# A recurrent layer on eight cores: layer-norm statistics in a pass of their own, eight PSUM banks for the projections, and half of the final stores from SP

## Chip, cores and metric

The kernel runs on all 8 cores of one Trainium2 chip. There are 2 sequences of 4096 tokens with 2048 channels; each core computes 1024 tokens of one sequence and reads 128 tokens (and one more) ahead of them, so that no core needs another's result. The metric is the device time in microseconds of the slowest core.

## What is computed

All weight matrices are 2048 x 2048. After a layer norm of x, the layer mixes each token with the one before it, makes four projections, runs a decaying scan over time, multiplies the result with two sigmoids, projects it again, normalises once more, and multiplies with a feed-forward branch whose weights are rounded to -1, 0 or 1.

```python
xn = _layernorm(x)
prev = jnp.concatenate([xn[:, 1:2, :], xn[:, :-1, :]], axis=1)
xx = prev - xn
r = (xn + xx * tm_r) @ Wr.T
k = (xn + xx * tm_k) @ Wk.T
v = (xn + xx * tm_v) @ Wv.T
g = sigmoid((xn + xx * tm_g) @ Wg.T)
w = exp(-exp(time_decay))
# scan over t:  ek = exp(k_t); out = (a + e^u*ek*v_t) / (b + e^u*ek)
#               a = w*a + ek*v_t;  b = w*b + ek
attn = sigmoid(r) * wkv
o = attn * g @ Wo.T
mu = o.mean(-1); var = ((o - mu) ** 2).mean(-1)
s = (o - mu) * rsqrt(var + 1e-5) * ln_g + ln_b
out = x + s * silu(xn @ ternary(W_ffn) + bias)
```

## The kernel before

Channels lie on the partitions (16 tiles of 128 channels, `CH` = 16) and the core's 1024 tokens (`T_OWN`) in the free dimension, as two chunks of 512 (`TC_OWN`). The program is a row of blocks. In a block each engine has its own hand-written list of instructions, and counting semaphores order them; a new block starts when all engines are through with the one before. All weights come from HBM in f32 and are cast to bf16 by ACT or VectorE (DVE) on the way into `wbf`.

The blocks are these. (1) Statistics of x: ACT makes an f16 copy and an f16 square of each tile, PE sums both over the partitions by matmuls with a column of ones. (2) Normalisation and mixing, the inputs of the projections written to HBM. (3) The projections k and v and the feed-forward branch, in `mm_group`. (4) The block that the change is mainly about (from line 732 on), called the rgo block here. (5) The final block (from line 1048 on).

The rgo block does three projections of 32 output groups each: p = 0 the receptance r (weights `wr`), p = 1 the gate g (`wg`), p = 2 the output o (`wo`). A group is 128 output channels by 512 tokens: 16 matmuls, one for each input tile, into one PSUM bank `ps[g % NBK]`, with NBK = 6 banks. Weights come in slabs of 512 output channels, four slabs to a projection and eight groups to a slab. Two slabs fit in `wbf`. SP loads a slab's 16 pieces of 128 x 512 f32 into two staging buffers `rgo_mw` (line 848), and ACT casts each (line 832, `emit_cast`). The cast of slab s+2 may start when PE is done with slab s, and it stands in ACT's list ahead of the first eviction of slab s+1. So ACT's order in a slab is: 16 casts, then eight evictions (lines 968, 975 and 978), each waiting for its group. PE waits before a group until ACT has evicted the group six before it.

During r, DVE also runs the scans, and ACT the Ln and Exp that make a reciprocal (lines 959, 961), two evictions apart. In the gate projection DVE multiplies each evicted chunk into `wkv_sb` (line 917), and PE starts the output projection only when all of that is done.

In the output projection ACT copies each group into `sr_sb` (line 978). After the second chunk of a channel tile it also makes that tile's f16 copy `oh16` (line 984) and f16 square `oq16` (line 986), two buffers of each. PE sums them over the partitions with four matmuls of a column of ones (`stats_mm`, lines 998 and 1001) into two more PSUM banks, `qsa` and `qsb`, one row per chunk. `stats_mm` of a tile stands in PE's list two tiles (four groups) later. At the end of the block DVE reads the sums and makes mean and variance, and ACT the reciprocal square root with Ln and Exp (lines 923 to 936 and 991 to 993).

```python
if (p == 2 and tj == ntc - 1
        and 0 <= sl * OSL + oc - 2):
    stats_mm(e, sl * OSL + oc - 2)
```

The final block broadcasts the two rows of statistics over the partitions (lines 1069 to 1091). Then for each of 16 channel tiles DVE scales and shifts o (lines 1123, 1126), ACT applies ln_g and ln_b (line 1097), and DVE multiplies with the feed-forward branch and adds x (lines 1110, 1113) into one of two buffers `outst`. SP loads x and the branch for tile ci (`xst`, line 1079; `g2ld`, line 1083) when tile ci-2 is done. POOL stores every tile to y (line 1136), and DVE waits before line 1110 for the store of the tile two before.

Of the kernel before, what the change touches and what calls it, by code (L numbers as in the profile page):

```python
# [8 lines left out]
F32 = mybir.dt.float32  # L9
# [6 lines left out]
LN_EPS = 1e-5  # L16
# [7 lines left out]
def build_nc(C, T_OWN, LANE):  # L24
# [15 lines left out]
           for k in ("wk", "wv", "wr", "wg", "wo", "wf")}  # L40
# [18 lines left out]
           ("sl", "sw0", "sw1", "scv", "scs", "smm", "sm2", "sev", "st0",  # L59
            "st1", "sv", "ss", "sden", "srd", "sg0", "sg1")}  # L60
# [633 lines left out]
    with contextlib.ExitStack() as es:  # L694
# [14 lines left out]
                     for i in range(8)]}  # L709
# [12 lines left out]
    oh16 = [es_o.enter_context(nc.sbuf_tensor("oh16_%d" % i, [128, T_OWN],  # L722
                                              F16)) for i in range(2)]
    oq16 = [es_o.enter_context(nc.sbuf_tensor("oq16_%d" % i, [128, T_OWN],
                                              F16)) for i in range(2)]
    stv = es_o.enter_context(nc.sbuf_tensor("stv", [1, T_OWN], F32))
    stm = es_o.enter_context(nc.sbuf_tensor("stm", [1, T_OWN], F32))
    stq = es_o.enter_context(nc.sbuf_tensor("stq", [1, T_OWN], F32))
# [3 lines left out]
    with contextlib.ExitStack() as es:  # L732
# [21 lines left out]
              for i in range(6)]  # L754
        qsa = ec(nc.psum_tensor("qsa", [128, 512], F32))
        qsb = ec(nc.psum_tensor("qsb", [128, 512], F32))
        qs1 = [qsa[32 * j:32 * j + 1, :] for j in range(len(TC_OWN))]
        qs2 = [qsb[32 * j:32 * j + 1, :] for j in range(len(TC_OWN))]
# [108 lines left out]
        def _(e):  # L867
# [53 lines left out]
            e.wait_ge(sem["sm2"], b["sm2"] + CH)  # L921
            for j, (t0, t1) in enumerate(TC_OWN):
                e.tensor_scalar(stm[:, t0:t1], qs1[j][:, :t1 - t0],  # L923
                                1.0 / C, None, OP.mult)
                e.tensor_scalar(stv[:, t0:t1], qs2[j][:, :t1 - t0],
                                1.0 / C, None, OP.mult)
            e.drain()
            e.tensor_tensor(stq[:, :], stm[:, :], stm[:, :], OP.mult)
            e.drain()
            e.tensor_tensor(stv[:, :], stv[:, :], stq[:, :], OP.subtract)  # L930
            e.drain()
            inc(e.tensor_scalar(stv[:, :], stv[:, :], LN_EPS, None,
                                OP.add), "sv")
            e.wait_ge(sem["ss"], b["ss"] + CH + 1)
            e.drain()
            inc(e.tensor_tensor(stm[:, :], stm[:, :], stv[:, :], OP.mult),
                "sv")
# [266 lines left out]
```

## Time and profile before

| | us |
|---|---|
| timed runs: lowest, median, highest of 2 | 1530.3, 1541.25, 1552.21 |
| the profiled execution, its own time | 1497.94 |
| its span, first to last instruction of the slowest core (core 4) | 1496.4 |
| spans of the eight cores | 1465.2 to 1496.4 |
| busy in that span: PE / DVE / ACT / POOL | 823.4 / 524.8 / 496.7 / 105.1 |

All times in the text are microseconds from the start of core 4's span, unless another core is named. By them the rgo block goes from 768 to 1394 (r to 1028, gate to 1210, output to 1380, then the end of the statistics) and the final block from there to the end. In the rows, PE is TensorE's matmuls, PEld its weight loads, DVE VectorE, ACT ScalarE, POOL GpSimd and SPq the DMA issues of SyncE. L1025 is line 1025 of the kernel. A row of a timeline is one instruction, or a run of equal ones (x96) with the time from the first to the end of the last; in brackets stands the engine's idle time ahead of it and what ended that.

### The profile page before, as it was taken

What the parts mean: (1) busy time and instruction counts of PE and PEld (TensorE: products, weight loads), DVE (VectorE), ACT (ScalarE), POOL (GpSimd) and SP (SyncE); (2) the same over time, 40 slices, a digit from 0 to 9 for tenths busy, and PEclk for the clock granted to TensorE, in tenths of its full rate; (3) what the DMA queues carried; (4) which work ended last, traced back from release to release, by engine and by line L of the source; (5) the groups of instructions that cost most, each with busy time, mean ns of one, the idle gap of its engine ahead of it and who ended that gap; (6) DMA issues with size and microseconds to landing.
All of it is one profiled execution on the core that took longest, in us unless ns stands there. A gap on an engine that the chain in (4) does not pass through costs nothing. (4 is left out here: it accounts for less than half of the span.)

```text
span 1496.4 us, 11814 instructions; the slowest of 8 cores (1465.2 to 1496.4 us)
## 1 busy us (share of the span) xinstructions
PE 823.4 (55%) x3834; PEld 359.4 (24%) x3834; DVE 524.8 (35%) x499; ACT 496.7 (33%) x660; POOL 105.1 (7%) x196
## 2 busy tenths in 40 slices
PE   3542210057938479999921758433766777569200
PEld 0110000023514145544410323111323332223000
DVE  0159998100000002765015149667100000000597
ACT  4532222112121121121212446745533235444221
POOL 0002222000000000011110001000000000000000
PEclk8555555578969689999975888676889998779555
DMA  4448879773361842654145443345333332320287
GB/s 128 126 149 261 264 244 261 164 228 113 109 164 53 249 123 90 182 165 140 39 148 175 120 128 111 98 145 172 85 113 110 94 100 76 85 85 1 83 253 226
DMA packets 79070, 211.65 MB, mean 141 GB/s; under 512 B 11424, under 2 KB 11424, under 8 KB 79008
## 3 DMA queue, kind: packets, MB, share of 16 engines
q1 hardware_dynamic: 54432, 139.57, 33.8%
q0 software_dynamic: 15360, 53.49, 9.9%
q10 hardware_dynamic: 9216, 17.83, 3.9%
q8 instruction: 31, 0.51, 0.1%
q14 instruction: 31, 0.25, 0.1%
HBM read 166.81 MB, written 39.85 MB: 138 GB/s over the span
## 5 line engine op out<-in xcount | busy, mean ns | idle before, releaser
L1025 PE MATMUL rgo_ps<-mov_rg,rgo_wbf 128*128 128x512 bf16 x1024 | 245.1, 405 | 204.5 <-ACT sr_sb L968 79.0
L405 PE MATMUL g1ps<-mov_kv,g1wbf 128*128 128x512 bf16 (+1 forms) x1536 | 259.5, 334 | 116.5 <-DMA mov_kv<-sxk 46.8
L832 ACT ACTIVATE rgo_wbf<-rgo_mw 128x512 bf16<-128x512 f32 x192 | 119.5, 629 | 273.8 <-DMA rgo_mw<-wr 89.7
L405 PEld LDWEIGHTS g1ps<-mov_kv,g1wbf 128*128 128x128 bf16 x1536 | 132.6, 100 | 243.3 <-issue 126.9
L1025 PEld LDWEIGHTS rgo_ps<-mov_rg,rgo_wbf 128*128 128x128 bf16 x1024 | 105.0, 103 | 344.6 <-issue 239.0
L1025 PE MATMUL rgo_ps<-wkv_sb,rgo_wbf 128*128 128x512 bf16 x512 | 116.9, 388 | 1.7 <-DVE wkv_sb L917 1.7
L405 PE MATMUL g1ps<-xn_sb,g1wbf 128*128 128x512 bf16 x512 | 110.8, 379 | 3.7 <-DVE g1wbf L266 3.7
L269 DVE CAST g1wbf<-g1mwstg 128x1024 bf16<-128x1024 f32 x24 | 16.7, 694 | 251.2 <-PE g1ps L405 94.7
L333 ACT ACTIVATE g1row<-g1ps 128x512 f16<-128x512 f32 (+1 forms) x96 | 44.5, 492 | 147.1 <-PE g1ps L405 135.4
L573 PE MATMUL ps_sc<-fs_a,ones 128*1 128x512 f16 x64 | 32.3, 609 | 86.9 <-ACT fs_a L618 86.9
L271 ACT ACTIVATE g1wbf<-g1mwstg 128x1024 bf16<-128x1024 f32 x24 | 25.4, 1056 | 127.6 <-DMA g1mwstg<-wv 76.3
L1025 PEld LDWEIGHTS rgo_ps<-wkv_sb,rgo_wbf 128*128 128x128 bf16 x512 | 49.9, 100 | 69.2 <-issue 14.5
L405 PEld LDWEIGHTS g1ps<-xn_sb,g1wbf 128*128 128x128 bf16 x512 | 50.0, 98 | 64.1 <-issue 4.1
L923 DVE TENSOR_SCALAR stm<-qsa 1x512 f32<-1x512 f32 x2 | 1.4, 680 | 172.8 <-PE qsb L1001 172.8
L618 ACT ACTIVATE fs_a<-g1mwstg 128x1024 f16<-128x1024 f32 x32 | 33.7, 1057 | 83.9 <-DMA g1mwstg<-wf 83.9
L901 DVE TENSOR_TENSOR wkv_sb<-r_vvr,r_ekr 128x1024 bf16<-128x1024 f16 x16 | 11.1, 692 | 136.6 <-ACT r_ekr L961 135.7
L917 DVE TENSOR_TENSOR wkv_sb<-wkv_sb,rgo_sg 128x512 bf16<-128x512 bf16 x32 | 13.6, 425 | 115.9 <-ACT rgo_sg L975 113.8
L340 ACT ACTIVATE g1g2s<-g1ps,v_bfv,scale_sb 128x512 bf16<-128x512 f32 x32 | 24.9, 777 | 85.5 <-PE g1ps L405 82.8
L261 DVE TENSOR_SCALAR g1mwm<-g1mwstg,thr_sb 128x1024 f32<-128x1024 f32 x32 | 24.1, 755 | 81.2 <-PE g1ps L405 52.0
L515 PE MATMUL ps<-xh,ones 128*1 128x512 f16 (+1 forms) x48 | 24.0, 499 | 34.7 <-ACT xq L502 34.7
L883 DVE TENSOR_TENSOR_SCAN zar<-w_sb,r_vvr 128x1152 f32<-128x1152 f32 x16 | 41.0, 2560 | 1.5 <-issue 0.4
L1136 POOL DMA_DIRECT2D y<-outst x16 | 8.5, 533 | 462.1 <-DVE outst L1113 462.1
(112 smaller groups left out, 861.4 us busy)
## 6 DMA issues: line engine op xcount, KB each, us to landing
g1mwstg<-wf SPq DMA_DIRECT2D x64, 512.0 KB, 5.0
g1mwstg<-wk SPq DMA_DIRECT2D x32, 512.0 KB, 7.2
g1mwstg<-wv SPq DMA_DIRECT2D x32, 512.0 KB, 5.0
rgo_mw<-wr SPq DMA_DIRECT2D x64, 256.0 KB, 3.3
rgo_mw<-wg SPq DMA_DIRECT2D x64, 256.0 KB, 3.3
rgo_mw<-wo SPq DMA_DIRECT2D x64, 256.0 KB, 3.4
xstg<-x SPq DMA_DIRECT2D x16, 576.5 KB, 3.8
xst<-x SPq DMA_DIRECT2D x16, 512.0 KB, 4.8
```

The lines of the kernel that those rows point to most:

```text
L261: e.tensor_single_scalar(mwm2[jj % 2][:, :], mwstg[jj % 2][:, :], thr_sb[:, :], OP.is_gt)
L269: e.tensor_copy(dstsl, mwstg[jj % 2][:, :]).then_inc(sem["scv"], 1)
L271: e.activation(dstsl, mwstg[jj % 2][:, :], AF.Copy).then_inc(sem["scs"], 1)
L333: inc(e.activation(rowst[ro % 2][:, t0:t1], bank[:, :t1 - t0], fn), "sev")
L340: inc(e.activation(g2st[gk % 2][:, :t1 - t0], bank[:, :t1 - t0], AF.Silu, bias=s["bias_vec"][:, ocg:ocg + 1], scale=scale_sb[:, 0:1]), "sev")
L405: mm = e.matmul(bank[:, :t1 - t0], wbf[hh % 2][:, ic, oc * 128:(oc + 1) * 128], s["mov"][:, ic, t0:t1], start=(ic == 0), stop=(ic == CH - 1))
L515: e.matmul(ps1[j][:, :t1 - t0], ones16[:, :], xh16[:, ci, t0:t1], start=(ci == 0), stop=(ci == CH - 1))
L573: mm = e.matmul(ps_sc[:, :q1 - q0], ones16[:, :], habs[sl_ % 2][:, q0:q1], start=(sl_ == 0 and j == 0), stop=(sl_ == NSL - 1 and j == len( ...
L618: inc(e.activation(habs[sl_ % 2][:, :], g1mwstg[sl_ % 2][:, :], AF.Abs), "scv")
L832: e.activation(wbf[ss % 2][:, ic, :], mwstg[jj % 2][:, :], AF.Copy).then_inc(sem["scs"], 1)
L883: e.tensor_tensor_scan(zar[:, 1:], wbc, vvr[m][:, :], 0.0, OP.mult, OP.add)
L1025: mm = e.matmul(bank[:, :t1 - t0], wbf[ss % 2][:, ic, oc * 128:(oc + 1) * 128], phs[p]["mov"][:, ic, t0:t1], start=(ic == 0), stop=(ic == ...
```

## The change

Four things change. The statistics leave the rgo block and get a block of their own behind it; the work in it is the same, tile by tile, with the same two buffers. The two PSUM banks that this frees go to the projections: NBK is 8. The semaphore `sm2` is gone and `smm` takes its part. In the final block the odd tiles are stored by SP (semaphore `sg0`), the even ones by POOL as before. The buffers of the statistics are allocated in the last part of the kernel.

```diff
         ps = [ec(nc.psum_tensor("rgo_ps%d" % i, [128, 512], F32))
-              for i in range(6)]
-        qsa = ec(nc.psum_tensor("qsa", [128, 512], F32))
-        qsb = ec(nc.psum_tensor("qsb", [128, 512], F32))
...
+              for i in range(8)]
...
                     inc(e.activation(sr_sb[:, ocg, t0:t1], bank[:, :t1 - t0],
                                      AF.Copy), "sev")
-                    if tj == ntc - 1:
-                        if ocg >= 2:
-                            e.wait_ge(sem["sm2"], b["sm2"] + ocg - 1)
-                        e.drain()
-                        e.activation(oh16[ocg % 2][:, :], sr_sb[:, ocg, :],
-                                     AF.Copy)
-                        inc(e.activation(oq16[ocg % 2][:, :],
-                                         sr_sb[:, ocg, :], AF.Square), "ss")
...
-                            if (p == 2 and tj == ntc - 1
-                                    and 0 <= sl * OSL + oc - 2):
-                                stats_mm(e, sl * OSL + oc - 2)
-            stats_mm(e, OSL * NSLAB - 2)
-            stats_mm(e, OSL * NSLAB - 1)
...
+            blk = esA.enter_context(nc.Block())
+            b = snap()
+
+            @blk.scalar
+            def _(e):
+                for ci in range(CH):
+                    if ci >= 2:
+                        e.wait_ge(sem["smm"], b["smm"] + ci - 1)
+                    e.activation(oh16[ci % 2][:, :], o_sb[:, ci, :], AF.Copy)
+                    inc(e.activation(oq16[ci % 2][:, :], o_sb[:, ci, :],
+                                     AF.Square), "ss")
...
+            @blk.tensor
+            def _(e):
+                for ci in range(CH):
+                    e.wait_ge(sem["ss"], b["ss"] + ci + 1)
+                    for j, (t0, t1) in enumerate(TC_OWN):
+                        e.matmul(ps1[j][:, :t1 - t0], ones16[:, :],
+                                 oh16[ci % 2][:, t0:t1],
+                                 start=(ci == 0), stop=(ci == CH - 1))
+                        mm = e.matmul(ps2[j][:, :t1 - t0], ones16[:, :],
+                                      oq16[ci % 2][:, t0:t1],
+                                      start=(ci == 0), stop=(ci == CH - 1))
+                    inc(mm, "smm")
...
                     inc(e.dma_start(g2ld[ci % 2][:, :], sg2[ci, :, :]),
                         "sw%d" % (ci % 2), 16)
+                    k = ci - 2
+                    if k >= 1 and k % 2 == 1:
+                        e.wait_ge(sem["sden"], b["sden"] + k + 1)
+                        inc(e.dma_start(y_d[k, :, :], outst[k % 2][:, :]),
+                            "sg0", 16)
...
-                    stp = "st%d" % (ci % 2)
+                    stp = "st0" if ci % 2 == 0 else "sg0"
...
-                for ci in range(CH):
+                for ci in range(0, CH, 2):
                     e.wait_ge(sem["sden"], b["sden"] + ci + 1)
                     inc(e.dma_start(y_d[ci, :, :], outst[ci % 2][:, :]),
-                        "st%d" % (ci % 2), 16)
+                        "st0", 16)
```

On ACT, in the output projection before, the second set of casts, the evictions behind it (`sr_sb<-rgo_ps`) and the f16 copies and squares (`oh`, `oq`) stand like this:

```order
L832 ACTIVATE rgo_wbf<-rgo_mw 128x512 x16
L978 ACTIVATE sr_sb<-rgo_ps 128x512 x2
L984 ACTIVATE oh_0<-sr_sb 128x1024
L986 ACTIVATE oq_0<-sr_sb 128x1024
L978 ACTIVATE sr_sb<-rgo_ps 128x512 x2
L984 ACTIVATE oh_1<-sr_sb 128x1024
L986 ACTIVATE oq_1<-sr_sb 128x1024
```

And in the changed kernel, from the last set of casts over the block boundary into the statistics:

```order
L821 ACTIVATE rgo_wbf<-rgo_mw 128x512 x16
L950 ACTIVATE sr_sb<-rgo_ps 128x512 x16
L725 UNCONDITIONAL_BRANCH
L1008 UNCONDITIONAL_BRANCH
L1013 ACTIVATE oh_0<-sr_sb 128x1024
L1014 ACTIVATE oq_0<-sr_sb 128x1024
L1013 ACTIVATE oh_1<-sr_sb 128x1024
L1014 ACTIVATE oq_1<-sr_sb 128x1024
```

The copies and squares have moved from between the evictions to behind all of them.

On PE, the output projection (`rgo_ps<-wkv_sb`) before, with the sums of the first two tiles among its groups:

```order
L1025 MATMUL rgo_ps<-wkv_sb,rgo_wbf 128x512 x96
L998 MATMUL qsa<-oh_0,ones 1x512
L1001 MATMUL qsb<-oq_0,ones 1x512
L998 MATMUL qsa<-oh_0,ones 1x512
L1001 MATMUL qsb<-oq_0,ones 1x512
L1025 MATMUL rgo_ps<-wkv_sb,rgo_wbf 128x512 x32
L998 MATMUL qsa<-oh_1,ones 1x512
```

And now, the whole of the gate and r projections in the first row and the whole output projection in the second:

```order
L974 MATMUL rgo_ps<-mov_rg,rgo_wbf 128x512 x1024
L974 MATMUL rgo_ps<-wkv_sb,rgo_wbf 128x512 x512
L725 UNCONDITIONAL_BRANCH
L1022 UNCONDITIONAL_BRANCH
L1027 MATMUL qs_0<-oh_0,ones 1x512
L1030 MATMUL qs_0<-oq_0,ones 1x512
L1027 MATMUL qs_1<-oh_0,ones 1x512
L1030 MATMUL qs_1<-oq_0,ones 1x512
```

Nothing stands between the output groups any more, and the sums follow behind a block boundary.

On SP, the end of the final block before (the loads of the last two tiles):

```order
L1079 DMA xst<-x 128x1024
L1083 DMA g2ld<-sg 128x1024
L1079 DMA xst<-x 128x1024
L1083 DMA g2ld<-sg 128x1024
L1048 UNCONDITIONAL_BRANCH
```

And now, with the stores of tiles 13 and 15:

```order
L1086 DMA xst<-x 128x1024
L1090 DMA g2ld<-sg 128x1024
L1086 DMA xst<-x 128x1024
L1090 DMA g2ld<-sg 128x1024
L1095 DMA y<-outst 128x1024
L1100 DMA y<-outst 128x1024
L1055 UNCONDITIONAL_BRANCH
```

A store of an odd tile has come in behind the two loads of the tile after next, and the last one closes SP's list.

## Rows read from the trace of the kernel before

**Rows 1.** Cores: span and mean granted TensorE clock of core 4.

```profile
core 4: 1496.4 us, clock 0.754
```

**Rows 2.** Windows of core 4: busy by engine (instructions), granted clock, DMA share, GB/s.

```profile
145.00:330.00 185.00, 32.96 (x110) 9.93 (x111) 112.49 (x98) 40.23 (x42) 31.39 (x59) 0.53 0.82 235
...
1085.00:1210.00 125.00, 89.60 (x384) 38.71 (x382) 10.60 (x25) 43.02 (x75) 0.00 (x0) 0.86 0.35 101
1210.00:1380.00 170.00, 125.19 (x572) 51.50 (x572) 0.04 (x1) 76.09 (x110) 0.00 (x0) 0.86 0.26 72
```

**Rows 3.** Timeline of ACT in the gate projection: evictions, then the next casts.

```profile
1157.64 3.02 ACT L975 ACTIVATE rgo_sg<-rgo_ps 128x512 bf16<-128x512 f32 x6
1164.22 0.60 ACT L975 ACTIVATE rgo_sg<-rgo_ps 128x512 bf16<-128x512 f32 x1 [3.57 <-PE rgo_ps L1025]
1167.68 0.60 ACT L975 ACTIVATE rgo_sg<-rgo_ps 128x512 bf16<-128x512 f32 x1 [2.86 <-PE rgo_ps L1025]
1168.17 1.14 ACT L832 ACTIVATE rgo_wbf<-rgo_mw 128x512 bf16<-128x512 f32 x2
```

**Rows 4.** Lines, 1085 to 1210: busy, mean ns, idle before and its releaser.

```profile
L975 ACT ACTIVATE rgo_sg<-rgo_ps 128x512 bf16<-128x512 f32 x25 | 13.2, 602 | 21.5 <-PE rgo_ps L1025 21.5
```

**Rows 5.** Timeline of PE at the start of the output projection.

```profile
1210.40 20.88 PE L1025 MATMUL rgo_ps<-wkv_sb,rgo_wbf 128*128 128x512 bf16 x96 [1.68 <-DVE wkv_sb L917]
1244.14 0.59 PE L998 MATMUL qsa<-oh,ones 128*1 128x512 f16 x2 [12.86 <-ACT oq L986]
...
1245.09 8.48 PE L1025 MATMUL rgo_ps<-wkv_sb,rgo_wbf 128*128 128x512 bf16 x32
```

**Rows 6.** Timeline of ACT in the receptance projection: first casts after the evictions.

```profile
918.72 1.15 ACT L832 ACTIVATE rgo_wbf<-rgo_mw 128x512 bf16<-128x512 f32 x2
```

**Rows 7.** Timeline of ACT, output projection: first cast and first eviction of each slab.

```profile
1209.36 1.14 ACT L832 ACTIVATE rgo_wbf<-rgo_mw 128x512 bf16<-128x512 f32 x2
...
1240.85 1.07 ACT L978 ACTIVATE sr_sb<-rgo_ps 128x512 bf16<-128x512 f32 x2
...
1256.27 1.13 ACT L832 ACTIVATE rgo_wbf<-rgo_mw 128x512 bf16<-128x512 f32 x2
...
1289.49 1.07 ACT L978 ACTIVATE sr_sb<-rgo_ps 128x512 bf16<-128x512 f32 x2
...
1304.48 1.13 ACT L832 ACTIVATE rgo_wbf<-rgo_mw 128x512 bf16<-128x512 f32 x2
...
1336.10 1.07 ACT L978 ACTIVATE sr_sb<-rgo_ps 128x512 bf16<-128x512 f32 x2
```

**Rows 8.** Timeline from the last statistics pair to the final block.

```profile
1379.93 1.06 ACT L984 ACTIVATE oh<-sr_sb 128x1024 f16<-128x1024 bf16 x1
1380.89 1.04 ACT L986 ACTIVATE oq<-sr_sb 128x1024 f16<-128x1024 bf16 x1
...
1382.80 0.68 DVE L923 TENSOR_SCALAR stm<-qsa 1x512 f32<-1x512 f32 x1 [172.76 <-PE qsb L1001]
...
1392.40 1.21 DVE L936 TENSOR_TENSOR stm<-stm,stv 1x1024 f32<-1x1024 f32 x1 [3.70 <-ACT stv L993]
1393.89 0.33 SPq L1079 DMA_DIRECT2D xst<-x  x1
```

**Rows 9.** Timeline of PE, 80 to 100: four matmuls with the ones column.

```profile
92.34 1.96 PE L573 MATMUL ps_sc<-fs_a,ones 128*1 128x512 f16 x4 [1.63 <-ACT fs_a L618]
```

**Rows 10.** Final block: instructions and waits of `outst`; one load's and one store's issue.

```profile
L1110 DVE TENSOR_TENSOR outst<-sstg,g2ld x16: 1224/1225/1226, 1410.6 to 1488.4; 128x1024 f32<-128x1024 f32 x16
...
  DMA y<-outst: 2.3, 4
...
DMA to landing us min/median/max: 3.0/6.5/7.5
...
1418.80 0.57 SPq L1083 DMA_DIRECT2D g2ld<-sg  x1
1418.95 0.54 POOL L1136 DMA_DIRECT2D y<-outst  x1 [4.66 <-DVE outst L1113]
```

More of the change, by code:

```diff
@@ L721, in build_nc @@
     es_o = contextlib.ExitStack()
[L722 to L728, printed above, removed]
     sr_sb = es_o.enter_context(
@@ L920, in _ @@
                                         OP.mult), "sv")
[L921 to L926, printed above, removed]
-            e.drain()
[L928 to L937, printed above, removed]
         @blk.scalar
@@ L1042, in build_nc @@
         ec = es.enter_context
+        oh16 = [ec(nc.sbuf_tensor("oh16_%d" % i, [128, T_OWN], F16))
+                for i in range(2)]
+        oq16 = [ec(nc.sbuf_tensor("oq16_%d" % i, [128, T_OWN], F16))
+                for i in range(2)]
+        stv = ec(nc.sbuf_tensor("stv", [1, T_OWN], F32))
+        stm = ec(nc.sbuf_tensor("stm", [1, T_OWN], F32))
+        stq = ec(nc.sbuf_tensor("stq", [1, T_OWN], F32))
         rb2 = ec(nc.sbuf_tensor("rb2", [128, T_OWN], F32))
@@ L1046, in build_nc, with _ @@
                for i in range(2)]
+        with contextlib.ExitStack() as esA:
+            ecA = esA.enter_context
+            ps1 = [ecA(nc.psum_tensor("qs1_%d" % j, [1, 512], F32))
+                   for j in range(len(TC_OWN))]
+            ps2 = [ecA(nc.psum_tensor("qs2_%d" % j, [1, 512], F32))
+                   for j in range(len(TC_OWN))]
+            blk = esA.enter_context(nc.Block())
[8 more added lines that the diff above has]
+                                     AF.Square), "ss")
+                e.wait_ge(sem["sv"], b["sv"] + 1)
+                e.activation(stv[:, :], stv[:, :], AF.Ln)
+                e.drain()
+                inc(e.activation(stv[:, :], stv[:, :], AF.Exp, scale=-0.5),
+                    "ss")
+            @blk.tensor
[10 more added lines that the diff above has]
+                    inc(mm, "smm")
+            @blk.vector
+            def _(e):
+                e.wait_ge(sem["smm"], b["smm"] + CH)
+                for j, (t0, t1) in enumerate(TC_OWN):
+                    e.tensor_scalar(stm[:, t0:t1], ps1[j][:, :t1 - t0],
+                                    1.0 / C, None, OP.mult)
+                    e.tensor_scalar(stv[:, t0:t1], ps2[j][:, :t1 - t0],
+                                    1.0 / C, None, OP.mult)
+                e.drain()
+                e.tensor_tensor(stq[:, :], stm[:, :], stm[:, :], OP.mult)
+                e.drain()
+                e.tensor_tensor(stv[:, :], stv[:, :], stq[:, :], OP.subtract)
+                e.drain()
+                inc(e.tensor_scalar(stv[:, :], stv[:, :], LN_EPS, None,
+                                    OP.add), "sv")
+                e.wait_ge(sem["ss"], b["ss"] + CH + 1)
+                e.drain()
+                inc(e.tensor_tensor(stm[:, :], stm[:, :], stv[:, :], OP.mult),
+                    "sv")
@@ L1084, in _ @@
                         "sw%d" % (ci % 2), 16)
+                    k = ci - 2
[3 more added lines that the diff above has]
+                            "sg0", 16)
+                for k in range(max(1, CH - 2), CH):
+                    if k % 2 == 1:
+                        e.wait_ge(sem["sden"], b["sden"] + k + 1)
+                        inc(e.dma_start(y_d[k, :, :], outst[k % 2][:, :]),
+                            "sg0", 16)
+                e.wait_ge(sem["sg0"], cnt["sg0"])
             @blk.scalar
```

22 lines of the change are left out of this document (2 added, 20 removed).

## Prediction, made before the changed kernel was run

> **What bounds the kernel now.** I read the cores first: the spans are close together (core 4 is the longest of 1465.2 to 1496.4 us) and TensorE was granted three quarters of its clock on average [rows 1]. No core is special. Then the busy times by stage: in the gate stage (1085 to 1210 us) and the output stage (1210 to 1380) PE is busy for 90 of 125 and 125 of 170 us, ACT for 43 and 76, DMA at 35% and 26% [rows 2]. Nothing is full there; two waits alternate. The ACT timeline shows how [rows 3]: after 16 casts of a weight slab come six evictions in 3.02 us, then 3.57 and 2.86 us of waiting for PE with one eviction behind each, then at once the next casts, at 1168.17. PE had stopped, because ACT evicts nothing while it casts and PE owns six banks: six groups, 20.88 us [rows 5], and it is out. Groups seven and eight start only after the casts, and the next casts only after them.
>
> **Part 1: eight banks in the gate stage.** With eight banks PE does a slab's eight groups under the casts. Six groups take 20.88 us, 3.48 each; two after a stall take 8.48 instead of 6.96 [rows 5]; so eight take 27.8 + 1.5 = 29.4 us. They start about 0.5 us after the casts of the slab before, when the first bank is free, and ACT asks for the results 4.0 us (eight evictions at 0.5) plus a set of casts later (from 1168.17 to 1209.36 a slab takes 41.2 us; less 6.4 of waiting and 4 of evictions that is 31): PE has 4 to 5 us to spare. What goes is ACT's wait for PE, 21.5 us over the stage in one row [rows 4], of which 3.57 + 2.86 = 6.4 lie in the slab shown. What is late next is the casts' own loads, which the change doesn't touch: a slab then costs 31 + 4 = 35 us. In the receptance stage before (818 to 1028 us) I cost the banks at nothing: ACT runs casts, Ln/Exp pairs with their table loads and sigmoids there without a gap, and the next casts start with no idle time ahead of them [rows 6], so PE is not waited for. **Term: -21.5 us** (ends 0 and -21.5: the wait cannot shrink below nothing).
>
> **Part 2: the output stage without the statistics.** Before, it runs from the first cast at 1209.36 to the end of the last eviction at 1379.9: 170.6 us [rows 7, 8]. In it are three sets of casts, from the rows 31.5, 33.2 and 31.6 us, 96.3 together [rows 7]. Between two sets lie eight evictions, four pairs of ACTIVATE for the statistics and PE's groups seven and eight, which PE starts only after the statistics matmuls that stand ahead of them: it waits 12.86 us for `oq` [rows 5]. After the change: 96.3 for the casts, two sets of eight evictions at 4.0, then the last slab: 0.5 until its first bank is free, 29.4 for its groups, 0.7 for the last eviction. 96.3 + 8.0 + 0.5 + 29.4 + 0.7 = 134.9 us. **Term: 134.9 - 170.6 = -35.7 us.** The pairs' removal is in this term.
>
> **Part 3: the statistics by themselves.** Before, 2.9 us lie between the start of the last pair and DVE's first read of the sums (1379.93 to 1382.80) [rows 8]. After, a block boundary comes first. Its price I take from the one that follows: DVE's last multiply ends at 1392.40 + 1.21, SP's first load starts at 1393.89, 0.3 us. Then 16 pairs on ACT alone. A pair's halves last 1.06 and 1.04 us and start 0.96 us apart, so a pair takes 1.91; 15 pairs 28.7 us, and the last one with its matmuls 2.9 as now. 0.3 + 28.7 = +29.0 us more than before. That holds with matmuls at the higher clock level. At the lower one (1.2 GHz) four matmuls of this shape last 1.96 us [rows 9], and with two `oh`/`oq` buffers the loop from a copy to the copy two tiles on is 0.96 + 1.04 + 1.96 + 0.2 of signalling = 4.16 us instead of 3.82: 16 x 0.17 = 2.7 us, and 1 us at the end. Ends +29.0 and +32.7. I take **+29.7 us**, near the warm end, since the pass starts warm from the last slab.
>
> The Trainium skill speaks to both parts on one page ("Perfetto Trace Analysis", Optimization Strategy). It advises interleaving regimes whose most-contended engine differs; the change undoes just that, and by this rule alone it would lose the pass, some 30 us. The same section says that the same gap coming back on an engine can mean too little PSUM for the next tile, and the ACT and PE rows are such a gap [rows 3, 5]. By the rows the second outweighs the first here.
>
> **Part 4: the odd stores.** In the last stage DVE is the limit: its first operation on a tile comes every 5.19 us (1410.6 to 1488.4, 15 steps), each of its four takes 1.23, and it waits only 2.3 us in all for a store [rows 10]. The eight odd tiles' stores move from POOL to SP, behind both loads of tile k+2, on the ring that carries those loads. POOL issued at 1418.95; SP is free of its second load at 1419.37, so the store goes 0.4 us later. Nobody is held up behind it: SP's next loads wait for DVE's next tile. DVE needs the buffer two tiles less two operations after the add, 10.4 - 2.5 = 7.9 us, 7.4 after POOL's issue; stores land 3.0 to 7.5 us after it, median 6.5 [rows 10]. So this is near an edge. Ends: -2.8 us (every wait for a store gone, and half a microsecond at the last store, which is odd and leaves SP at once) and +14 (the ring serves the store after the loads: 0.9 of issue, 6 for the loads, 3.0 for the store, 9.9 us against 7.9 allowed, 2 us for each of seven). **Term: -0.5 us**, the last store alone, because the bytes stay the same and DVE keeps its 5.2 us a tile.
>
> The skill's "DMA: Bandwidth & Descriptors" (Issuing engines are not separate DMA queues) says that transfers of all issuing engines run on the same 16 engines and a second issuer saves issue time only. By it the bandwidth gain of part 4 is zero; no row here shows a store from SP.
>
> **Sum.** -21.5 - 35.7 + 29.7 - 0.5 = -28.0 us. The profiled execution took 1497.9 us, so it would take 1469.9. The two timed runs took 1530.3 and 1552.2, 32 to 54 more, for a reason that the trace does not hold. The terms are sums of fixed counts of instructions, so I take the same 28.0 from the median 1541.25: 1513.2 us, 1.8% less. Faster or slower by 2%, 30.8 us, is about what a measurement of this kernel can tell from no change.
>
> **Rivals.** *A, the small terms fall well*: the statistics matmuls stay warm (+29.0), the store waits go (-2.8). -21.5 - 35.7 + 29.0 - 2.8 = -31.0, 1510.2 us, just past 2%. For it: each term is inside its bounds. Against: it needs both.
> *B, the stores on SP's ring hold up DVE*: +14 instead of -0.5, so -13.5 us, 1527.7. For it: the slowest store already lands when it is needed. Against: on one ring a store no longer shares its turn with the loads that follow it.
> *C, the loads set the slab's length; this one ends slower.* A slab is 16 loads of 256 KB, 4.19 MB: 102 GB/s in the 41.2 us of now, 120 in 35. If eight cores cannot load faster than they do now, the casts stretch until a slab takes as long as before. Then the gate term is gone and, of the output term, its first two slabs: from cast to cast 46.9 and 48.2 us against 35.5 and 37.2 after the change, 22.4 us. The last slab's 13.3 stays: -13.3 + 29.7 - 0.5 = +15.9, 1557.2 us. It decides from 28 / 7 = 4 us of stretch in each of the seven sets of casts. Against it: the core moved 101 GB/s in the gate stage, and 235 at 145 to 330 us, where the other cores loaded too [rows 2]. To reach 2% slower it must also meet B.
> *D, PE is too slow for the banks to help*: at the lower level a group of 16 matmuls would take about twice 3.48 us and eight 56, longer than the casts. Against: the pair after a stall loses 1.5 us in all [rows 5], so it is back at the higher level within a group. Its price would be above that of C.
>
> **Chances.** My forecast 0.50, A 0.25, B 0.12, C and D 0.08, others 0.05. Faster by over 2% is A and a quarter of the forecast, which lies 2.8 us from the line: 0.38. Slower by over 2% takes the worst of C and D: 0.05. The rest, 0.57, is within 2%. The executions seen differ by 54 us among themselves; so the range goes from the midpoint of the profiled and the lowest timed run less the gain, 1514 - 28 = 1486, to B with 12 us of the same spread, 1540.
>
> **What would show it.** Right: in the gate stage 16 casts, eight evictions in 4.0 us, casts again, no wait for PE, slabs 35 us apart; an output stage of about 135 us; a statistics stretch of about 31 us with ACT back to back; DVE's tile still 5.2 us in the last stage. Wrong: sets of casts of 35 us or more (C); waits of DVE for `y` above 1 us on odd tiles (B); ACT waiting for PE in the statistics stretch (the cold end of part 3); groups of 7 us (D).

## The result, and the profile after

| | before | after |
|---|---|---|
| timed, median (runs) | 1495.61 (10) | 1462.36 (11) |
| lowest to highest | 1489.41 to 1552.21 | 1447.38 to 1503.14 |
| profiled execution, its own time | 1497.94 | 1465.46 |
| its span, slowest core | 1496.4 | 1463.9 |
| its span, median of the eight cores | 1476.4 | 1445.1 |

The changed kernel takes 0.9731 of the time before, interval 0.9690 to 0.9773: 2.7% faster, some 40 us. The forecast was 1513.2 with a range from 1486 to 1540; the measured 1462.4 lies outside it. The gain was forecast as 28 us. The base it was taken from, 1541.25, was the median of two runs (1530.3 and 1552.2) that turned out to be the two highest of ten. In some executions two to four cores of one die run 20 to 80 us longer than the others, at granted clocks down to 0.69 (six of 57 later executions of the kernel before took 1529 to 1554 us in this way), and the ratios leave such disturbed executions out, four of the changed kernel's eleven here, which is why the ratio says 40 us where the medians of all runs differ by 33.

The gate stage on ACT in the changed kernel, from the timeline of core 4 (start, duration, engine, line and operation); the rows with single casts between are left out. It answers to [rows 3]:

```profile
1118.89 4.00 ACT L947 ACTIVATE rgo_sg<-rgo_ps 128x512 bf16<-128x512 f32 x8
1122.70 1.21 ACT L821 ACTIVATE rgo_wbf<-rgo_mw 128x512 bf16<-128x512 f32 x2
...
1153.24 4.00 ACT L947 ACTIVATE rgo_sg<-rgo_ps 128x512 bf16<-128x512 f32 x8
1157.05 1.21 ACT L821 ACTIVATE rgo_wbf<-rgo_mw 128x512 bf16<-128x512 f32 x2
...
1187.43 4.00 ACT L947 ACTIVATE rgo_sg<-rgo_ps 128x512 bf16<-128x512 f32 x8
```

Eight evictions stand in one row of 4.00 us, with no bracket ahead of them: ACT found its groups done each time. Before there were six and then two waits. From one first eviction to the next it is 34.4 and 34.2 us; the prediction said 35.

The output projection on PE, and its end on ACT, same core. It answers to [rows 5, 7]:

```profile
1192.57 29.64 PE L974 MATMUL rgo_ps<-wkv_sb,rgo_wbf 128*128 128x512 bf16 x128 [8.44 <-ACT rgo_wbf L821]
1222.45 27.79 PE L974 MATMUL rgo_ps<-wkv_sb,rgo_wbf 128*128 128x512 bf16 x128 [0.23 <-ACT sr_sb L950]
1256.87 29.92 PE L974 MATMUL rgo_ps<-wkv_sb,rgo_wbf 128*128 128x512 bf16 x128 [6.63 <-ACT sr_sb L950]
1290.65 29.47 PE L974 MATMUL rgo_ps<-wkv_sb,rgo_wbf 128*128 128x512 bf16 x128 [3.87 <-ACT sr_sb L950]
```

PE now does a whole slab, 128 matmuls, in one stretch of 27.8 to 29.9 us (29.4 was forecast), where it broke off after 96. It waits for ACT only between slabs. The windows of core 4 for the gate stage, the output stage, the statistics and the final block (busy time and count by engine, granted clock, DMA share, GB/s), beside [rows 2]:

```profile
1088.00:1191.00 103.00, 82.44 (x358) 35.78 (x356) 11.18 (x27) 41.73 (x74) 0.00 (x0) 0.91 0.40 123
1191.00:1321.00 130.00, 116.82 (x512) 51.11 (x512) 1.02 (x3) 46.43 (x81) 0.00 (x0) 0.94 0.33 93
1321.00:1355.00 34.00, 18.45 (x64) 4.71 (x64) 0.64 (x2) 31.77 (x33) 0.00 (x0) 0.90 0.00 0
1376.00:1464.00 88.00, 0.00 (x0) 0.00 (x0) 77.98 (x64) 19.84 (x16) 4.27 (x8) 0.50 0.72 221
```

The output stage takes 130 us for the matmuls that took 170; its rate of loading rises from 72 to 93 GB/s because the same bytes move in less time. The third row is the new pass: ACT busy for 31.8 of 34 us, and the DMA engines idle. How it begins and ends, with the rows that answer to [rows 8]:

```profile
1320.22 0.60 ACT L950 ACTIVATE sr_sb<-rgo_ps 128x512 bf16<-128x512 f32 x1 [2.86 <-PE rgo_ps L974]
...
1321.08 1.28 ACT L1013 ACT_TABLE_LOAD   x1 [0.26 <-PEq L725]
1322.38 1.06 ACT L1013 ACTIVATE oh<-sr_sb 128x1024 f16<-128x1024 bf16 x1
...
1326.49 1.06 ACT L1013 ACTIVATE oh<-sr_sb 128x1024 f16<-128x1024 bf16 x1 [0.22 <-PE qs L1030]
...
1354.36 0.68 DVE L1039 TENSOR_SCALAR stm<-qs 1x512 f32<-1x512 f32 x1 [162.16 <-PE qs L1030]
...
1360.26 1.06 ACT L1017 ACTIVATE stv<-stv 1x1024 f32<-1x1024 f32 x1 [7.17 <-DVE stv L1048]
...
1362.59 1.21 DVE L1052 TENSOR_TENSOR stm<-stm,stv 1x1024 f32<-1x1024 f32 x1 [2.42 <-ACT stv L1019]
...
1364.07 0.33 SPq L1086 DMA_DIRECT2D xst<-x  x1
```

Between the last eviction and DVE's first read lie 33.5 us. ACT waits for PE once, for 0.22 us. A table load (ACT loading its function tables) that the prediction had not counted stands ahead of the first copy; in exchange the one ahead of the logarithm (line 991 before) is gone, and the row work up to the last multiply is 1.4 us shorter.

Each stage's length, as the median of the eight cores, in us. "r" is the time up to the end of the receptance evictions; "statistics" runs from the last eviction to DVE's first read of the sums; "rows" is the mean and variance work; "tail" is from DVE's last add to the end of the span. The medians need not add up.

| | r | gate | output | statistics | rows | broadcast, final | tail |
|---|---|---|---|---|---|---|---|
| before | 1011.2 | 180.1 | 167.2 | 2.9 | 10.8 | 98.0 | 5.3 |
| after | 1013.1 | 158.2 | 129.6 | 33.6 | 9.4 | 98.6 | 3.0 |
| difference | +1.9 | -21.9 | -37.6 | +30.7 | -1.4 | +0.6 | -2.3 |
| forecast | 0 | -21.5 | -35.7 | +29.7 | 0 | 0 | -0.5 |

### The profile page after: what moved, and what is told of

It is laid out like the page before. It is cut to its first block and busy times, and to the rows that moved or that the text cites. A ratio compares the mean times of both kernels' runs of the same rounds, so it can differ in the third digit from the quotient of the medians.

```text
span 1463.9 us, 11807 instructions; the slowest of 8 cores (1437.9 to 1463.9 us)
## 1 busy us (share of the span) xinstructions
PE 827.9 (57%) x3834; PEld 362.3 (25%) x3834; DVE 524.4 (36%) x499; ACT 494.0 (34%) x660; POOL 101.8 (7%) x188
## 5 line engine op out<-in xcount | busy, mean ns | idle before, releaser
L974 PE MATMUL rgo_ps<-mov_rg,rgo_wbf 128*128 128x512 bf16 x1024 | 235.8, 395 | 189.7 <-ACT rgo_wbf L821 121.5
L269 DVE CAST g1wbf<-g1mwstg 128x1024 bf16<-128x1024 f32 x24 | 16.7, 694 | 246.6 <-PE g1ps L405 94.4
L515 PE MATMUL ps<-xh,ones 128*1 128x512 f16 (+1 forms) x48 | 24.0, 499 | 34.2 <-ACT xq L502 34.2
L874 DVE TENSOR_TENSOR_SCAN zbr<-w_sb,r_ekr 128x1152 f32<-128x1152 f32 x16 | 40.5, 2533 | 0.0
```

The source lines that it names most:

```text
L515: e.matmul(ps1[j][:, :t1 - t0], ones16[:, :], xh16[:, ci, t0:t1], start=(ci == 0), stop=(ci == CH - 1))
L874: e.tensor_tensor_scan(zbr[:, 1:], wbc, ekr[m][:, :], 0.0, OP.mult, OP.add)
L974: mm = e.matmul(bank[:, :t1 - t0], wbf[ss % 2][:, ic, oc * 128:(oc + 1) * 128], phs[p]["mov"][:, ic, t0:t1], start=(ic == 0), stop=(ic == ...
```

## The experiments

Unless it says otherwise an edit is made to the changed kernel. "Median core" is the median of the eight cores' spans, averaged over the executions that the ratio keeps; where profiles are named, it is that of the one profiled execution. Why it is used follows from the next three runs. A stage's length is always its median over the cores in the profile.

### The same programs again: three runs on the base

No edit, twice the changed kernel and once the kernel before.

> The changed kernel once more, beside the kernel before on one chip, to size the effect by cores and not by the slowest one alone. Theory F (the step times of the profiles are the whole effect): the median over the eight cores falls by what the two profiled executions differ, 1476.4 - 1445.1 = 31 us, and the time of the slowest core by 31 to 33. Rival N (the slowest core is picked by chance among eight, and the before-kernel's slowest core stands out more): the median core falls by 31, the slowest by about 40, as in the timed runs so far (1495 to 1455).

Measured: 1459.65 against 1490.16, ratio 0.9816 [0.9754, 0.9879]: 1.8% faster, not 2.7% as in the first comparison. The median core went from 1472.5 to 1440.3, 32.2 less. The stages repeat the first profile's within some 3 us (output 132.8, gate 159.6, statistics 33.5).

> The kernel before, unchanged, against itself, to see what this measurement calls a difference, and to have its eight cores' spans in timed runs. If the timed effect of the change (27 us on one chip, 40 on another) is larger or smaller than the 31 us of the median core only by chance of the slowest core, the ratio is 1 within 0.8%, the median core lies at 1473 to 1478 us in each fast run and the slowest core 10 to 25 us above it. Rival: the timed runs' median core stands apart from the profiled one's, by more than 5 us; then the profile understates the effect.

Measured: 1493.34 against 1493.04, ratio 0.9992 [0.9949, 1.0036]. A program against itself comes out within half a per cent, so neither 0.9731 nor 0.9816 comes from the way of comparing.

> The changed kernel a third time, beside the run of the kernel before against itself. Step times of the profiles: median core 31 us under that of before, fast runs' ratio 0.979 +- 0.006. Rival (an effect of 40 us as in the first comparison): 0.973 or less.

Measured: 1460.19 against 1493.04, ratio 0.9801 [0.9761, 0.9841]; median core 1444.6 against 1475.4, 30.8 less. The three comparisons give gains of 40, 27 and 30 us by the slowest core, and 31 to 32 by the median core (profiles and the last two). The slowest core lies 3 to 25 us above the median one, and it is another core from run to run: at the median 10 us in 39 executions of the kernel before, and 15 in 19 of the changed one. So the kernel's own gain is 31 us; what the timed metric adds or takes is that scatter. Whether the gain passes 2% stays open: of the three intervals only the first lies wholly beyond it. The median of the kernel before is 1487 to 1496 in all four comparisons (the fourth stands beside the later experiments); only single executions reach 1541.

### Six and seven banks

```diff
-              for i in range(8)]
+              for i in range(6)]
```

and `range(7)` in the second.

> The changed kernel with six banks for the projections instead of eight; everything else as changed. Theory F (the banks carry the gain, the split costs): ACT waits for PE again in each slab, 6.4 us. Against the changed kernel +2.2 + 3 x 6.4 in the gate stage = +21, and in the output stage two slabs at +6.4 and the last with groups seven and eight of the slab before still to do, +7: +20. So about 41 us slower than the changed kernel, and 2 to 9 us slower than the kernel before. Rival S (taking the statistics out from between the output groups is what pays, because ACT and PE no longer wait for each other there): the output stage stays within 10 us of the changed kernel's 130 us and the kernel is at least 20 us faster than before.

> The changed kernel with seven banks. Theory F: one group, 3.5 us, is left outside the casts in each slab, but ACT's first seven evictions (3.5 us) overlap the start of it; per slab 16 casts, seven evictions, a wait of 2.9 to 4 us for the eighth group, one eviction: +3.5 us a slab against eight banks. Six slabs with a next set of casts, 3.5 each, and 3.5 in the last: +21 to +25 us against the changed kernel. Rival E (seven are enough, since the wait ends when ACT starts evicting and PE has 4 to 5 us to spare): within 5 us of the changed kernel.

Six banks: 1502.64, ratio 1.0123 [1.0063, 1.0183]: slower than the kernel before. Against the changed kernel the median core is 39.4 longer in the profiles, of which 20.4 in the gate stage and 20.9 in the output stage. The waits are back in ACT's timeline (core 1):

```profile
1151.93 3.02 ACT L947 ACTIVATE rgo_sg<-rgo_ps 128x512 bf16<-128x512 f32 x6
1158.83 0.60 ACT L947 ACTIVATE rgo_sg<-rgo_ps 128x512 bf16<-128x512 f32 x1 [3.89 <-PE rgo_ps L974]
1162.29 0.60 ACT L947 ACTIVATE rgo_sg<-rgo_ps 128x512 bf16<-128x512 f32 x1 [2.86 <-PE rgo_ps L974]
1162.78 1.14 ACT L821 ACTIVATE rgo_wbf<-rgo_mw 128x512 bf16<-128x512 f32 x2
```

Seven banks: 1483.47, ratio 0.9926 [0.9873, 0.9979], the gate stage 10.4 and the output stage 10.6 longer than with eight. Each bank is worth 10 us in each stage, and rivals S and E fall. This splits the change: the banks give -41, and moving the statistics out (with the odd stores from SP), with no bank gained for it, would by itself have cost about 10 us (+30.8 for the pass, -1.4 in the rows, -2.3 in the tail, and 167.2 to 150.5 = -16.7 in the output stage; the span medians say +8). The timed runs put both higher: their median core is 1489.3 with six banks, in three executions, which makes -49 for the banks and +17 for the rest. The split is known to some 10 us, the sum of 31 better.

### The kernel before with a seventh bank

The four rows of sums go into one bank, and the freed one to the projections.

```diff
-              for i in range(6)]
+              for i in range(7)]
...
-        qsb = ec(nc.psum_tensor("qsb", [128, 512], F32))
...
-        qs2 = [qsb[32 * j:32 * j + 1, :] for j in range(len(TC_OWN))]
+        qs2 = [qsa[64 + 32 * j:65 + 32 * j, :] for j in range(len(TC_OWN))]
```

> The kernel BEFORE with one edit: the four rows of statistics share one PSUM bank (rows 0, 32, 64, 96), and the projections have seven banks. The statistics stay between the output groups. Theory O (order): the gate stage falls by 10 us, as from six to seven banks in the changed kernel, but the output stage does not move, because in PE's list the sums of a tile whose copy ACT makes only after the casts stand ahead of the seventh group: PE stops after six groups whatever the banks. So 10 us less than before. Rival P (banks alone): the output stage falls by 10 us too, 20 us less than before.

Measured: 1473.91, ratio 0.9893 [0.9848, 0.9937], median core 1462.4 against 1475.2. So this small edit alone gives some 13 us. The gate stage is 13.4 shorter, the output stage only 2.5: rival P falls. The same bank is worth 10.3 in the output stage once the statistics are out (140.2 against 150.5). PE's timeline of core 4 shows why:

```profile
1184.49 20.88 PE L1024 MATMUL rgo_ps<-wkv_sb,rgo_wbf 128*128 128x512 bf16 x96 [1.69 <-DVE wkv_sb L916]
1217.48 0.58 PE L997 MATMUL qsa<-oh,ones 128*1 128x512 f16 x1 [12.11 <-ACT oq L985]
1217.48 0.59 PE L1000 MATMUL qsa<-oq,ones 128*1 128x512 f16 x1
1217.48 0.58 PE L997 MATMUL qsa<-oh,ones 128*1 128x512 f16 x1
1217.49 0.59 PE L1000 MATMUL qsa<-oq,ones 128*1 128x512 f16 x1
1218.01 9.31 PE L1024 MATMUL rgo_ps<-wkv_sb,rgo_wbf 128*128 128x512 bf16 x32
```

PE has a free bank after 96 matmuls and still stops for 12 us: next in its list stand the statistics of a tile whose square ACT makes only after its casts. The list's order stops it, and no bank helps there. So a bank and the removal of the statistics are worth more together than apart; that is shown for the seventh bank, not for the eighth, for which the interleaved form has no room.

### All stores from POOL again

```diff
-                    k = ci - 2
-                    if k >= 1 and k % 2 == 1:
-                        e.wait_ge(sem["sden"], b["sden"] + k + 1)
-                        inc(e.dma_start(y_d[k, :, :], outst[k % 2][:, :]),
-                            "sg0", 16)
...
-                for ci in range(0, CH, 2):
+                for ci in range(CH):
```

> The changed kernel with all sixteen stores of y issued by POOL, as before the change. Theory F: only the end differs. In the profiles the time from DVE's last addition to the end of the span is 5.4 us with the last store from POOL and 3.0 us with it from SP, so +2.4 us, and DVE keeps its 5.2 us a tile. Rival Q (SP's share of the stores relieves the ring or POOL, so that loads land earlier: 4.2 us against 4.8 for x): DVE's waits come back too, +5 us or more, and x lands in 4.8 us again.

Measured: 1463.3, ratio 0.9842 [0.9779, 0.9904]. From DVE's first operation on a tile to its last add it is 86.4 against 86.8; only the tail differs, 5.1 instead of 3.0. Last rows of this kernel (core 7), and then of the changed one (core 4):

```profile
1459.85 1.23 DVE L1120 TENSOR_TENSOR outst<-outst,xst 128x1024 f32<-128x1024 f32 x1 [0.45 <-issue]
1461.63 0.53 POOL L1143 DMA_DIRECT2D y<-outst  x1 [4.39 <-DVE outst L1120]
```

```profile
1457.14 0.53 POOL L1154 DMA_DIRECT2D y<-outst  x1 [9.94 <-DVE outst L1131]
1457.81 1.23 DVE L1128 TENSOR_TENSOR outst<-sstg,g2ld 128x1024 f32<-128x1024 f32 x1 [1.22 <-DMA y<-outst]
1459.48 1.23 DVE L1131 TENSOR_TENSOR outst<-outst,xst 128x1024 f32<-128x1024 f32 x1 [0.45 <-issue]
1460.78 0.34 SPq L1100 DMA_DIRECT2D y<-outst  x1
```

From the end of the add to the issue it takes POOL 0.55 us and SP 0.07. The store lands 2.9 us after the issue in both. The rest of the 2.1 us comes after the landing: the program ends 1.6 us later with POOL, of which 1.35 are a drain on POOL, and 0.3 later with SP. DVE's waits for a store are hardly touched. On every core of all three kernels DVE waits at the last tile, for 1.1 to 2.8 us in the changed kernel, 1.3 to 2.6 here and 1.4 to 2.9 before; the waits of the whole block add up to 1.1 to 4.6, 1.3 to 3.7 and 2.0 to 4.5. Rivals B and Q both fall: the waits do not grow by 14 us with SP's stores, nor do they come back with POOL's.

### What the statistics pass is made of

First, without the f16 copy. The sum of o is taken from the bf16 tile itself, so that its rounding differs; the squares stay.

```diff
-                    e.activation(oh16[ci % 2][:, :], o_sb[:, ci, :], AF.Copy)
...
-                        e.matmul(ps1[j][:, :t1 - t0], ones16[:, :],
-                                 oh16[ci % 2][:, t0:t1],
+                        e.matmul(ps1[j][:, :t1 - t0], onesb[:, :],
+                                 o_sb[:, ci, t0:t1],
```

> The changed kernel without the f16 copy of o in the statistics: PE sums the bf16 tile itself, with a bf16 column of ones; ACT makes the squares alone. Theory A (ACT paces the pass, 1.89 us a pair): a tile costs one square, 0.95 us, so the stretch from the last eviction to the first read of the sums falls from 33.6 to 18.5 us, 15 less, if the four matmuls of a tile stay 0.21 us apart (0.86 us). Rival L (PE falls to its lower clock level when it waits in every tile): 1.7 to 1.9 us a tile, the stretch stays above 30 us, and nothing is gained.

Measured: 1450.57, ratio 0.9675 [0.9623, 0.9727]. The pass takes 22.2 us instead of 33.6 (21.1 to 23.6 over the cores), and neither of the expected lengths. ACT's timeline (core 7, whose pass is the shortest; six more such rows follow):

```profile
1307.66 2.00 ACT L1013 ACTIVATE oq<-sr_sb 128x1024 f16<-128x1024 bf16 x2
1309.98 2.00 ACT L1013 ACTIVATE oq<-sr_sb 128x1024 f16<-128x1024 bf16 x2 [0.32 <-PE qs L1029]
```

A square takes 1.04 us and starts 0.96 after the one before when ACT is free. Here two start every 2.32 us, 1.16 each, with a wait of 0.32 for PE ahead of every pair. With two buffers a square may start only when PE has summed the tile two before. With the copy gone ACT is fast enough for that to hold it up. To see whether it is the buffers, the next kernel, this one with one more edit, has four of them.

```diff
-                for i in range(2)]
+                for i in range(4)]
...
-                    if ci >= 2:
-                        e.wait_ge(sem["smm"], b["smm"] + ci - 1)
+                    if ci >= 4:
+                        e.wait_ge(sem["smm"], b["smm"] + ci - 3)
...
-                                      oq16[ci % 2][:, t0:t1],
+                                      oq16[ci % 4][:, t0:t1],
```

> The changed kernel without the f16 copy, with four buffers for the squares instead of two. Without the copy the statistics stretch took 22.2 us, not 18.5, and PE began a new pair of tiles every 2.32 us, 1.16 a tile, at the higher clock level. Theory Z (a loop through two buffers: 1.04 for the square, 0.14 to PE, 0.86 for its matmuls, 0.2 back, per two tiles): with four buffers ACT runs back to back and a tile costs 0.95, so 18.5 to 19.5 us. Rival (PE or its signalling paces it at 1.16 a tile): 22 us again.

Measured in one execution: the pass takes 18.6 us, 3.6 less, and ACT waits once (core 3):

```profile
1298.81 5.93 ACT L1013 ACTIVATE oq<-sr_sb 128x1024 f16<-128x1024 bf16 x6
1305.39 9.75 ACT L1013 ACTIVATE oq<-sr_sb 128x1024 f16<-128x1024 bf16 x10 [0.65 <-PE qs L1029]
```

So the two buffers were the loop. Its time of 1430.95, a single one, is no comparison.

Last, the pass is taken apart: DVE, idle in the output stage, squares each finished tile into `mov_rg`, and PE sums the tiles and the squares behind its last group, 64 matmuls in all, into banks already evicted. ACT's copies and squares go, and their block with them (not shown in the diff). The squares are bf16 here.

```diff
+            for ci in range(CH):
+                e.wait_ge(sem["sev"], b["sev"] + NRG + (ci + 1) * ntc)
+                inc(e.tensor_tensor(mov_rg[:, ci, :], sr_sb[:, ci, :],
+                                    sr_sb[:, ci, :], OP.mult), "sv")
...
+            e.wait_ge(sem["sev"], b["sev"] + NG - NBK + 4)
+            for ci in range(CH):
+                e.wait_ge(sem["sv"], b["sv"] + NSV + ci + 1)
```

> The changed kernel with the statistics back in the rgo block in another form: DVE, idle in the output stage, squares each tile (bf16, into mov_rg, which is free by then); PE sums the bf16 tiles and the squares after its last group, into banks that are evicted by then; no work on ACT, no block boundary. Theory A: the stretch from the last eviction to the first read of the sums falls from 33.6 us to the 64 matmuls at 0.21 us, 13.8, less what runs beside the last eviction: 13 to 15 us. The table load of Ln comes back into the row part (+1.3). So 17 to 19 us less than the changed kernel and 45 to 50 less than before. Rival B2 (DVE's squares get in the way of ACT's evictions or of the casts): the output stage grows over 131 us and takes part of it back.

Measured: 1443.95, ratio 0.9673 [0.9627, 0.9718]; the pass is 13.3 us, as expected, the output stage 129.5 as in the changed kernel (rival B2 falls), and the rows 1.3 longer, since the table load goes back ahead of the logarithm. PE starts its sums while ACT still evicts the last group (core 7), and a matmul follows every 0.215 us:

```profile
1316.27 0.38 PE L1017 MATMUL rgo_ps<-sr_sb,onesb 128*1 128x512 bf16 x1
1316.44 0.60 ACT L978 ACTIVATE sr_sb<-rgo_ps 128x512 bf16<-128x512 f32 x1 [2.85 <-PE rgo_ps L1006]
1316.49 0.38 PE L1020 MATMUL rgo_ps<-mov_rg,onesb 128*1 128x512 bf16 x1
...
1317.14 0.69 DVE L919 TENSOR_TENSOR mov_rg<-sr_sb 128x1024 bf16<-128x1024 bf16 x1 [6.21 <-ACT sr_sb L978]
```

64 x 0.215 = 13.8: what is left of the pass is PE alone. DVE squares a tile in 0.69 us where ACT's copy and square take 1.9.

### What sets a slab's length now

In the changed kernel ACT's casts wait for their loads: in the output stage for 59 of 130 us, by this row of the lines of core 4, 1191 to 1321 (busy, mean ns, idle before and its releasers).

```profile
L821 ACT ACTIVATE rgo_wbf<-rgo_mw 128x512 bf16<-128x512 f32 x48 | 30.1, 637 | 61.3 <-DMA rgo_mw<-wo 59.0 <-PE rgo_ps L974 1.9
```

Rival C puts that down to the cores' common rate of loading. The other explanation is that only two loads of 256 KB are in flight. Four staging buffers tell the two apart.

```diff
+        NST = 4
...
-                 for i in range(2)]
+                 for i in range(NST)]
...
-            e.wait_ge(sem["sw%d" % (jj % 2)], swtarget[jj])
+            e.wait_ge(sem["sw%d" % (jj % NST)], swtarget[jj])
...
-                if jj >= 2:
-                    eng, sname, tgt = castrec[jj - 2]
+                if jj >= NST:
+                    eng, sname, tgt = castrec[jj - NST]
```

> The changed kernel with four staging buffers for the weight pieces in the rgo block instead of two, each with its own semaphore. Theory W (with eight banks a slab is a set of casts plus four us of evictions, and the casts wait for loads that are only two deep): the wait of 3 us for each pair goes; a set of casts falls from 31 us to between 10 (ACT alone, 16 x 0.63) and 18 us (4.19 MB at the 235 GB/s seen elsewhere); gate and output slabs fall from 35 to the 28 to 30 us that PE needs, 5 us each for six slabs; the receptance stage falls from 55 us a slab to the 42 us of DVE's four scans, 4 x 13 us; the first two sets of casts by 20. In all 80 to 110 us less than the changed kernel. Rival H (the eight cores together take all that the memory gives, my rival C): the sets stay near 31 us and the time stays.

Measured: 1351.7, ratio 0.9095 [0.9052, 0.9139]. Median core 105 us below the changed kernel in the profiles: r 56, gate 32, output 17. C falls. ACT at the turn from gate to output (core 0), and the window from 1009 to 1150:

```profile
1036.23 2.17 ACT L823 ACTIVATE rgo_wbf<-rgo_mw 128x512 bf16<-128x512 f32 x4
1041.94 2.65 ACT L823 ACTIVATE rgo_wbf<-rgo_mw 128x512 bf16<-128x512 f32 x4 [3.53 <-DMA rgo_mw<-wg]
...
1056.36 3.02 ACT L949 ACTIVATE rgo_sg<-rgo_ps 128x512 bf16<-128x512 f32 x6
1059.91 0.60 ACT L949 ACTIVATE rgo_sg<-rgo_ps 128x512 bf16<-128x512 f32 x1 [0.53 <-PE rgo_ps L976]
1063.36 0.60 ACT L949 ACTIVATE rgo_sg<-rgo_ps 128x512 bf16<-128x512 f32 x1 [2.86 <-PE rgo_ps L976]
```

```profile
1009.00:1150.00 141.00, 138.63 (x634) 63.03 (x645) 10.43 (x25) 69.67 (x123) 0.00 (x0) 1.00 0.52 150
```

Casts come up to four at a time and this set takes 20.1 us (1036.2 to 1056.4) where it took 30.5 (1122.7 to 1153.2 in the rows of the changed kernel). ACT waits for PE again, but now because PE is full: 138.6 of 141 us, at a granted clock of 1.00. The core loads 150 GB/s where it loaded 123. A load lands after 4.0 us at the median instead of 3.3, so each takes longer with more of them under way, but by far less than their number grows. These are the rows of the tile `rgo_mw` between 1009 and 1150 us, time from issue to landing; first the changed kernel (core 4), then this one (core 0):

```profile
DMA to landing us min/median/max: 3.0/3.3/8.0
```

```profile
DMA to landing us min/median/max: 3.0/4.0/6.6
```

### Four staging buffers and DVE's squares together

The two edits of the last kernels in one.

> Four staging buffers and the statistics with DVE's squares, together. The two touch different stretches: e7 fell by 105 us against the changed kernel (median core 1445 to 1340), e8 by 16. If they add, the median core is at 1324 and the time at 1330 to 1336, ratio 0.895 to 0.90 against before. Rival: with slabs of 28 us, DVE's squares and the output groups share less idle time, and PE's sums wait for ACT's last evictions; then the gain of e8 shrinks below 10 us.

Measured: 1331.65 (1319.35 to 1339.87), ratio 0.8919 [0.8870, 0.8968]. The two gains add up: in the profiles the median core is 1318.7, against 1339.7 and 1429.3 with one edit alone, so the squares by DVE give 21 us here and 16 there, and the rival falls. It is faster than both kernels of this study, 10.8% below the one before. Its bf16 squares are a change of precision in the variance.

## Why the prediction was right and wrong

**The failing step** is in the sum: "The terms are sums of fixed counts of instructions, so I take the same 28.0 from the median 1541.25". The 28.0 were counted in a profiled execution of 1497.9 us, and the two timed runs lay 32 to 54 above it "for a reason that the trace does not hold". Given that, the profiled execution was the better base. It lies 2.3 us from the median later measured, 1495.6. From it the forecast would have been 1469.9, which is 7.5 above the measured 1462.4, and a range of the same width, 27 us to each side, would have held it. The range's low end, 1486, came from the midpoint of the two bases, and so left the right one out. That before belongs at 1487 to 1496 is shown by four comparisons with 10 to 17 runs each. Executions of this height came back now and then, as said under the result; whether the first two were of that kind stays open, since the record has no spans of their cores. The forecast gain itself, 28 us, stands against 31 in the median core; most of its terms and the mechanism behind them held.

**Gate stage**: right. -21.9 for -21.5 (-20.5 on core 4, whose rows the term came from), and ACT's wait for PE in it is gone. The runs with six and seven banks show the cause: 20.4 come back with two banks fewer. That r gains nothing held too (+1.9).

**Output stage**: right in kind, 1.9 short at the median (-37.6 for -35.7) and 5.3 short on core 4, from which the term was taken: 129.6 us there where 134.9 was worked out. The three sets of casts took 91.0 instead of 96.3, which is all of it, and PE's last slab 29.5 for 29.4. The change did not shorten the sets. Over the eight cores the three take 89.2 to 97.8 us before (median 91.4) and 89.6 to 95.0 after (median 91.3), and core 4 had the second longest before. So the error lies in reading one core: with 91.4 the same working gives 130.0 us and, from the median 167.2, -37.2.

**Statistics pass**: 1.0 too low. It measures +30.7 for +29.7. Of that the table load ahead of the first copy makes 1.28, and it was missing from the sum. That it "starts warm" was wrong: PE had idled for 4.4 us, the granted clock is 0.50, the lower level, from 1323 to 1329 us and 1.00 from 1330 to 1354, and matmuls start 0.43 us apart at first and 0.21 later. But this lasts for three tiles and costs ACT one wait of 0.22. The Trainium skill ("ScalarE: Activation LUTs", What ACT_TABLE_LOAD costs) gives 1283 ns for such a load; the trace agrees, 1.28. With it counted at the new place and struck at the old one, both this term and the rows' -1.4 come out within 0.5 us.

**Odd stores**: -2.3 for -0.5, inside the bounds of -2.8 and +14, but for another reason than the waits those allowed for. About 0.5 of it is the earlier issue, as predicted; most of the rest is POOL's closing work after its last store, which I had not looked for at the end of the trace of before. The sign named for rival B, a wait above 1 us on an odd tile, was a bad one: tile 15 has such a wait on every core, before the change too.

**The rivals.** A's time, 31 us less, is what the median core shows (31.3 in the profiles, 32.2 and 30.8 timed), by other terms than A named: the matmuls did not stay warm and the store waits did not go, so that the agreement is luck. B: refuted, the final block stays within 1 us and DVE's waits with it. C: refuted twice, by slabs of 34 us after the change and by 105 us from two more buffers. D: refuted, a slab's groups take 29.6 us.

**Interleaving or banks.** The Trainium skill's advice to interleave ("Perfetto Trace Analysis", Optimization Strategy) pulled the other way than the same section's remark on too little PSUM. The runs now separate them. Undoing the interleaving alone (six banks, statistics apart) costs some 8 us by the profiles and 17 by the timed runs; the banks give 39 and 49. And the kernel with a seventh bank shows the price of interleaving in a list kept in order: the bank gave 2.5 us where it gives 10.

## What to carry to other kernels

Count a change in one profiled execution and put the result on that execution's time, but take each term's price from more than one core. When few timed runs disagree with it, the range must hold both bases. Before adding work to an engine's fixed list between large pieces, ask what stands behind it: here a stalled small matmul stopped PE for 12 us with a bank free. And where an engine waits "for DMA" while the DMA engines are busy for a third of the time, count the transfers in flight first: two more buffers gave three times what the studied change did.

## What was not expected of the hardware

- Four matmuls of a column of ones into rows 0, 32, 64 and 96 of one bank start within 0.01 us and end together, 0.60 us after the first start behind a wait of 12 us and 0.39 within the stage (the kernel before with a seventh bank). Into rows 0 and 32 of two banks they start in two pairs, 0.21 us apart (the kernel before, at 1382.1 us).
- The program ends 2.1 to 2.3 us sooner when the last store comes from SP and not from POOL. Of this 1.35 lie behind the landing.
- Each of the seven blocks begins with a table load on ACT (1.28 us); in two of them, at 300.4 and 1321.1 us of the changed kernel, the activations just before and just after the load are both plain copies. The second of these loads serves the logarithm of its block too.
- The slowest of eight cores running one program is 3 to 25 us above the median one, and not always the same; three comparisons gave 27 to 40 us for a gain that the median core puts at 31 to 32.
